# Token-by-token queries and keys in the last stage of a three-stage kernel, with longer loops on the matmul engine

## What is computed

```python
h = einsum('bhid,oi,od->bho', x, weighted_sum, weight)   # image tokens
h = concatenate([h, txt], axis=1)
h = h + attn(layernorm(h))     # 16 heads of 16; for each token position the 8 batch rows attend to each other
h = h + ffn(layernorm(h))

def ffn(x):                    # "last stage" below
    h = rmsnorm(x, gamma1)
    q = (h @ Wq + bq).reshape(b, t, H, HD)
    kv = ((h @ Wdown + bdown) @ Wup + bup).reshape(b, t, H, 2 * HD)
    k, v = split(kv, 2, axis=-1)
    att = softmax(einsum('bthd,btgd->bthg', q, k) / sqrt(HD))   # heads of one token attend to each other
    out = einsum('bthg,btgd->bthd', att, v).reshape(b, t, D)
    x = x + (out @ Wo + bo)
    h2 = rmsnorm(x, gamma2)
    gate = softmax(h2 @ Wg + bg)
    return x + einsum('btd,edf,bte->btf', h2, We, gate)         # 8 experts
```

## Time and profile before

| | us |
|---|---|
| median of 3 runs | 808.26 (807.35 to 809.14) |
| the profiled execution | 807.2 |
| its span (first to last instruction) | 805.3 |
| PE busy | 764.3 |
| DVE busy | 663.1 |
| POOL busy | 405.5 |
| ACT busy | 374.0 |

### The profile page before, as it was taken

How to read it: one execution, slowest core, us unless ns; L and a number is a source line. 1 busy time by engine, 2 the same in 40 slices (tenths; PEclk the granted TensorE clock), 3 DMA queues, 4 the chain that set the end, 5 groups by cost and what they waited for, 6 DMA issues and landing times.

```text
span 805.3 us, 48234 instructions
## 1 busy us (share of the span) xinstructions
PE 764.3 (95%) x20274; PEld 532.5 (66%) x20274; DVE 663.1 (82%) x1591; ACT 374.0 (46%) x985; POOL 405.5 (50%) x1094
## 2 busy tenths in 40 slices
PE   4999979999999998878999999999999999999998
PEld 3888845677677675566656666666666666666664
DVE  5798676899999997767778778778778877877877
ACT  4477444565666565534433434434333343443321
POOL 1231354566665667534545555555565565555311
PEclk9999998999999999978999999999999999999999
DMA  9987000000000000000001001001101100100100
GB/s 331 333 239 226 3 3 4 2 0 0 0 0 0 0 0 2 16 13 17 26 20 26 19 20 26 23 16 26 26 13 26 26 19 20 26 23 17 29 15 20
DMA packets 38377, 33.25 MB, mean 41 GB/s; under 512 B 24786, under 2 KB 33570, under 8 KB 38314
## 3 DMA queue, kind: packets, MB, share of 16 engines
q1 hardware_dynamic: 38314, 32.35, 13.4%
HBM read 22.64 MB, written 4.83 MB: 34 GB/s over the span
## 4 chain that ended last, share of the span: by engine, by line
PE 59%; DVE 16%; issue 8%; POOL 3%; DVEq 1%; ACT 0%; POOLq 0%; ACTq 0%
PE bank L192 13%; PE bank L194 11%; PE bank L193 11%; PE bank L957 9%; PE bank L968 6%; DVE smax L435 2%; DVE k_t L466 2%; DVE ss L469 2%; PE bank L976 1%; DVE qn L460 1%; DVE q_t L464 1%; PE bank L995 1%; DVE on_t_l L444 1%; PE bank L275 1%; DVE on L428 1%
## 5 line engine op out<-in xcount | busy, mean ns | idle before, releaser
L192 PE MATMUL bank<-we_h,h_t_h 128*128 128x512 f16 x296 | 112.9, 382 | 1.1 <-DVE res L1277 0.9
L193 PE MATMUL bank<-we_l,h_t_h 128*128 128x512 f16 x296 | 112.2, 379 | 0.0
L194 PE MATMUL bank<-we_h,h_t_l 128*128 128x512 f16 x296 | 112.2, 379 | 0.0
L1277 DVE SCALAR_TENSOR_TENSOR acc<-bank,gate,acc 128x256 f32<-128x256 f32 x222 | 101.9, 459 | 3.9 <-PE bank L194 3.4
L1286 DVE TENSOR_REDUCE smax<-bank 128x16 f32<-128x512 f32 x37 | 25.6, 692 | 70.7 <-PE bank L957 70.7
L192 PE MATMUL bank<-tokw_h,x_t_h 128*128 128x256 f16 x256 | 70.8, 277 | 11.3 <-DVE x_t_l L690 11.3
L957 PEld LDWEIGHTS bank<-kv_t,fq_t 32*32 32x32 f32 x4736 | 71.3, 145 | 10.7 <-issue 10.7
L957 PE MATMUL bank<-kv_t,fq_t 32*32 32x32 f32 x4736 | 76.0, 225 | 1.8 <-issue 1.7
L193 PE MATMUL bank<-tokw_l,x_t_h 128*128 128x256 f16 x256 | 70.8, 277 | 0.0
L194 PE MATMUL bank<-tokw_h,x_t_l 128*128 128x256 f16 x256 | 70.8, 276 | 0.0
L968 PEld LDWEIGHTS bank<-fpr_t,v 32*32 32x32 f32 x4736 | 48.2, 104 | 22.9 <-issue 22.1
(11 more groups left out here) (223 smaller groups left out, 2243.0 us busy)
## 6 DMA issues: line engine op xcount, KB each, us to landing
xbuf<-in_x SPq DMA_DIRECT2D x32, 512.0 KB, 5.2
out<-res SPq DMA_DIRECT2D x36, 128.0 KB
we_s<-in_we SPq DMA_DIRECT2D x4, 512.0 KB, 7.1
inw<-in_in_w SPq DMA_DIRECT2D x1, 768.0 KB, 11.8
hn_t_h<-hn_r_h SPq DMA_TRANSPOSE x37, 2.3
hn_t_l<-hn_r_l SPq DMA_TRANSPOSE x37, 2.4
wrep<-in_w_rep SPq DMA_DIRECT2D x1, 512.0 KB, 4.4
h_all<-in_txt SPq DMA_DIRECT2D x1, 512.0 KB
```

The source lines that it names most:

```text
L192: nc.tensor.matmul(dst, a_h(c), b_h(c), start=start and c == 0, stop=False)
L193: nc.tensor.matmul(dst, a_h(c), b_l(c), start=False, stop=False)
L194: last = nc.tensor.matmul(dst, a_l(c), b_h(c), start=False, stop=stop and c == chunks - 1)
L1277: nc.vector.scalar_tensor_tensor(out=(res if e == E - 1 else acc)[:, :], in0=b_we[s % 2][:, k * D:(k + 1) * D], scalar=gate[p][:, e:e + 1] ...
```

## The change

Three things are changed.

1. In the last stage `fq_t` and `kv_t` lie token by token. A pair is now tokens 2p and 2p + 1. `fq_t` holds 16 heads of a token in a run, so the stationary operand is one run of 32 words; the transpose that writes it steps by 16 words from element to element. `kv_t` keeps its content (the same flat order), but is read with both tokens of a pair next to each other: 16 runs of 2 words, 32 words apart. The transposes into `v48` and `of` and the mask follow suit.
2. PE's loops: attention covers turns 2 to 33, the last stage 4 to 35. Turn 39, which is empty, goes (`end=`). For that the wait for `bvec` moves to turn 1 and the wait for `a_h` is dropped; instead DVE does `added` ahead of on_l, so that `a_onl` covers both.
3. Normalised rows of tiles 0, 1 and 2: ACT writes them at the end of turns 32, 33, 34; POOL's low halves for them stand at the start of its turns 33, 34 and 35, ahead of Newton's steps; `first_coefficients` comes in turns 28 to 31.

```diff
--- before.py
+++ after.py
@@ -36,7 +36,6 @@
 XT = 3
 MIX = 4
 MIX0 = 3
-HEAD = range(TILES - 4, TILES + 2)
 JOIN = TILES - 1
 AHEAD = 4
 WS = 256.0
@@ -61,7 +60,7 @@
     eng.wait_ge(sem, 1)
 
 
-def tiles_in_order(eng, body, back, ahead, unroll=2, last_ahead=None, start=None, tail=None):
+def tiles_in_order(eng, body, back, ahead, unroll=2, last_ahead=None, start=None, tail=None, end=None):
 
 
     first = -(-(back + 1) // unroll) * unroll
@@ -71,7 +70,7 @@
     with eng.Fori(first // unroll, first // unroll + turns) as g:
         for p in range(unroll):
             body(g * unroll + p, p)
-    for i in range(first + unroll * turns, TILES + back):
+    for i in range(first + unroll * turns, end or TILES + back):
         if tail:
             tail(i)
         else:
@@ -317,6 +316,8 @@
                 sums(i, p, 1)
 
             def rows(i, p):
+                if isinstance(i, int) and i == 1:
+                    pe.wait_ge(bvec_ready, 1)
                 if real(i, 2):
                     pe.wait_ge(a_xtl, i + 3)
                     wait(pe, a_qk, i + 1)
@@ -335,9 +336,6 @@
                     last.then_inc(a_xnps, 1)
                 if real(i, -2):
                     pe.wait_ge(a_onl, i - 1)
-                    wait(pe, a_h, i - 2)
-                    if isinstance(i, int) and i == 2:
-                        pe.wait_ge(bvec_ready, 1)
                     rows_times(b_out, on_h, on_l, lambda c: outw_h[:, c, :], lambda c: outw_l[:, c, :]).then_inc(a_out, 1)
 
             def body(i, p):
@@ -440,12 +438,13 @@
                                             ALU.subtract).then_inc(a_sub, 1)
                 if real(i, -2):
                     dve.wait_ge(a_onh, i - 1)
+                if real(i, -3):
+                    added(i - 3)
+                if real(i, -2):
                     wait(dve, a_out, i - 2)
                     nc.vector.tensor_tensor(on_l[:, :, :], b_ot[:, 0:D], on_h[:, :, :], ALU.subtract).then_inc(a_onl, 1)
                 if early:
                     divisor(i)
-                if real(i, -3):
-                    added(i - 3)
                 if real(i, 0):
                     dve.wait_ge(a_exp, i + 1)
 
@@ -842,7 +841,7 @@
         hn_r = [halves(f"hn_r{p}", [P, D]) for p in range(2)]
         fpr_t = sb("fpr_t", [P, H, 32])
         fq_t = sb("fq_t", [P, 32, H])
-        kv_t = sb("kv_t", [P, 32, 16])
+        kv_t = sb("kv_t", [P, H, 32])
         of = sb("of", [P, H, 32])
         x2 = sb("x2", [P, D])
         hx2 = [sb(f"hx2_{p}", [P, D]) for p in range(2)]
@@ -955,8 +954,8 @@
                     for j in range(4):
                         q = slice(32 * j, 32 * j + 32)
                         last = nc.tensor.matmul(b_s3[q, pair * 32:pair * 32 + 32],
-                                                fq_t[q, :, pair],
-                                                kv_t[q, :, pair],
+                                                fq_t[q, 2 * pair:2 * pair + 2, :].rearrange("r t h -> r (t h)"),
+                                                kv_t[q, :, 2 * pair:2 * pair + 2],
                                                 start=False, stop=True, skip_group_check=True)
                 return last
 
@@ -1212,14 +1211,13 @@
             def join(i):
 
                 p, t = i % 2, i - JOIN
-                if t in (-3, -2):
+                if t in (-4, -3, -2):
                     a_body(i, p)
-                    rows(t, p)
+                    rows(t + 1, 1 - p)
                 elif t == -1:
                     asked(t)
                     down(t)
                     a_body(i, p)
-                    rows(t, 1)
                 elif t == 0:
                     asked(t)
                     down(t)
@@ -1319,7 +1317,7 @@
                 combine(i, p, 0)
                 if real(i, 1):
                     dve.wait_ge(f_qpad, i + 2)
-                    nc.vector.transpose(fq_t[:, :, :].rearrange("r (h t) p -> r h (t p)", t=2), qpad[:, :, :])
+                    nc.vector.transpose(fq_t[:, :, :].rearrange("r t h -> r h t"), qpad[:, :, :])
                 combine(i, p, 1)
                 if real(i, -1):
                     dve.wait_ge(f_wo, i)
@@ -1332,15 +1330,15 @@
                 combine(i, p, 2)
                 if real(i, 1):
                     dve.wait_ge(f_kv, i + 2)
-                    nc.vector.transpose(kv_t[:, :, :].rearrange("r n p -> r (n p)"), b_kv[:, :]).then_inc(f_kvt, 1)
+                    nc.vector.transpose(kv_t[:, :, :], b_kv[:, :]).then_inc(f_kvt, 1)
                 combine(i, p, 3)
                 if real(i, 1):
                     dve.wait_ge(f_kvt, i + 2)
                     nc.vector.transpose(v48[1 - p][:, :, 0:32],
-                                        kv_t[:, :, :].rearrange("r n p -> r p n")).then_inc(f_qt, 1)
+                                        kv_t[:, :, :].rearrange("r g (p t) -> r p g t", t=2)).then_inc(f_qt, 1)
                 if real(i, 0):
                     dve.wait_ge(f_av, i + 1)
-                    nc.vector.transpose(of[:, :, :], b_o3[:, :].rearrange("r (p h t) -> r h t p", h=H, t=2)).then_inc(f_of, 1)
+                    nc.vector.transpose(of[:, :, :], b_o3[:, :].rearrange("r (t h) -> r h t", h=H)).then_inc(f_of, 1)
                 combine(i, p, 4)
                 if real(i, 0):
                     dve.wait_ge(f_of, i + 1)
@@ -1379,7 +1377,13 @@
             return body, join
 
         def ffn_pool(pool):
-            def body(i, p):
+            def low(i, p):
+
+                if real(i, 3):
+                    pool.wait_ge(f_hn, i + 4)
+                    nc.gpsimd.tensor_tensor(hn_r[1 - p][1][:, :], hn[1 - p][:, :], hn_r[1 - p][0][:, :], ALU.subtract).then_inc(p_hnl, 1)
+
+            def body(i, p, early=None):
                 if real(i, 1):
                     pool.wait_ge(f_qraw, i + 2)
                     wait(pool, f_qt, i + 1)
@@ -1403,13 +1407,12 @@
                     pool.wait_ge(f_x1, i + 1)
                     wait(pool, f_x2, i)
                     nc.gpsimd.tensor_tensor(x1b[:, :], x1[:, :], bo_s[:, :], ALU.add).then_inc(p_x1, 1)
-                if real(i, 3):
-                    pool.wait_ge(f_hn, i + 4)
-                    nc.gpsimd.tensor_tensor(hn_r[1 - p][1][:, :], hn[1 - p][:, :], hn_r[1 - p][0][:, :], ALU.subtract).then_inc(p_hnl, 1)
+                if early is None:
+                    low(i, p)
                 if real(i, AHEAD) and real(i, 0):
                     ffn_coefficients(pool, i + AHEAD)
 
-            return body
+            return body, low
 
 
 
@@ -1418,8 +1421,8 @@
             @block.tensor
             def _(pe):
                 turn, (body, join) = attn_pe(pe)[0], ffn_pe(pe)
-                tiles_in_order(pe, turn, 3, 3, last_ahead=4, start=-1, tail=join)
-                tiles_in_order(pe, body, 2, 3, start=3)
+                tiles_in_order(pe, turn, 1, 3, start=-1, tail=join, end=TILES + 2)
+                tiles_in_order(pe, body, 2, 1, start=3)
 
             @block.scalar
             def _(act):
@@ -1437,16 +1440,20 @@
             def _(pool):
                 coefficients(pool, early, IMG_TILES)
 
-                body, head = attn_pool(pool), ffn_pool(pool)
+                body, (head, low) = attn_pool(pool), ffn_pool(pool)
 
                 def tail(i):
 
-                    body(i, i % 2)
-                    if HEAD[0] - 4 <= i < HEAD[0]:
-                        first_coefficients(pool, i - HEAD[0] + 4)
-                    if i in HEAD:
-                        turn = i - HEAD[0] - 3
-                        head(turn, turn % 2)
+                    p, t = i % 2, i - JOIN
+                    if t in (-3, -2, -1):
+                        low(t, p)
+                    body(i, p)
+                    if t < -4:
+                        first_coefficients(pool, t + 8)
+                    if t == -1:
+                        head(t, p, True)
+                    if t in (0, 1, 2):
+                        head(t, p)
 
                 tiles_in_order(pool, body, 3, 3, start=-1, last_ahead=8, tail=tail)
                 tiles_in_order(pool, head, 2, 3, last_ahead=AHEAD, start=3)
@@ -1505,7 +1512,7 @@
         "wo": a["L0_ffn_Wo"], "g2": columns(a["L0_ffn_gamma2"]),
         "wg": a["L0_ffn_Wg"], "we": a["L0_ffn_We"],
         "ident_c": np.eye(P, dtype=np.float32),
-        "amask_c": mask(4, lambda n: n % 32 // B, lambda n: n % 32 // B), "fmask_c": mask(2, lambda n: n % 2, lambda n: n % 2),
+        "amask_c": mask(4, lambda n: n % 32 // B, lambda n: n % 32 // B), "fmask_c": mask(2, lambda n: n % 32 // 16, lambda n: n % 2),
         "bv": columns(a["L0_attn_in_proj_bias"][2 * D:]), "bo": a["L0_ffn_bo"], "bq": a["L0_ffn_bq"], "bg": a["L0_ffn_bg"],
         "biases": np.concatenate([a["L0_attn_in_proj_bias"], a["L0_attn_out_b"], a["L0_ffn_bq"], a["L0_ffn_bo"], a["L0_ffn_bg"],
                                   np.zeros(P * BC - NBIAS, np.float32)]).reshape(P, BC),
```

## The result

The changed kernel takes 773.19 us (median of 4 runs, 771.31 to 774.41) where the kernel before takes 807.81 (4 runs): ratio 0.957, 95% interval 0.954 to 0.961. The forecast was 780 (780.2 by its sum) with a range from 774 to 797. The profiled execution took 773.28 us, its span is 771.3.

What follows compares the result with a forecast made beforehand. PE was taken to set steady last-stage turns, DVE steady attention turns. From 807.2 us, -21.8 (scores) - 4.0 - 1.8 - 0.7 (loops) + 0.2 (rows) = -28.1 gave 779.1, or 780.2 as median; range 774 to 797.

Steps and rivals of the forecast that it cites:

- I take 1.37, the nearest row in shape and count: 0.59 saved per turn: Last stage's score burst: falls from 1.96 to the sums' 1.37 us, 37 x 0.59 = 21.8 us saved.
- Bounds for one burst: Last stage's score burst: 1.96 us if nothing changes, 1.37 if it equals the sums' burst.
- more from the loops than I took (772 to 775): PE's loops: a larger saving than forecast, total 772 to 775 us, chance 0.04.
- The rival on the weight side: Score burst: only the weight side was the cost, half of 0.59 saved, 10.9 lost, 791 us; chance 0.17.
- DVE's price: DVE's last-stage transposes: fq_t rises from 0.70 to 1.03 us, v48 falls from 1.03 to 0.70, net zero.
- The slower rival: Last stage: fq_t's stepped write makes DVE the end; at 3.5 us the total is 820; chance 0.04.
- The loops: PE's loop bounds: 4.0 at attention's exit, 1.8 at its entry, 0.7 at the last loop's exit saved.
- Turns 4 and 5: Attention loop's entry: these turns, 6.41 and 7.58, come from the loop at 12.2 together, 1.8 us saved.
- The exit: Attention turns 32 to 35: 34.2 us falls to 30.2, 4.0 saved (0 to 6.6).
- Turn 34 becomes the first behind the loop and gets the stall: Attention turn 34: takes the stall and the low clock, 9.0 us; 6.6 saved at the exit if it stays clean.
- The last exit: Last stage's loop exit: the 1.18 us stall moves from turn 34 to 36, 0.7 us saved (0 to 1.4).
- worth nothing by itself: Attention turn 35: removing PE's 2.33 us wait for the halves saves nothing alone, as POOL's chain ends the turn.

Runs made afterwards that it cites:

- e1: The kernel before with only the token-by-token fq_t and kv_t layout and its transposes and mask; 781.30 us, ratio 0.964.
- e3: The changed kernel with kv_t read with a step of 16 words again, fq_t still in one run; 796.01 us, ratio 0.984.
- e4: The changed kernel with fq_t read with a step of 16 words again, kv_t still in pairs; 797.61 us, ratio 0.985.
- e2: The changed kernel with the fq_t and kv_t layout undone, loops and rows kept; 800.55 us, ratio 0.988.
- e6: The changed kernel with both PE loops at their old bounds (4 to 31, 4 to 33); 780.73 us, ratio 0.967.
- e7: The changed kernel with PE's attention loop over turns 4 to 33 and the last stage's loop as before; 782.19 us.
- e8: The changed kernel with PE's attention loop over turns 2 to 31 and the last stage's loop as before; 781.10 us.
- e10: The changed kernel with v48 widened to a pitch of 64 words, so the sums' weights start at multiples of 32 words; 771.10 us.
- e15: The changed kernel with transposed probabilities written so that the sums read them as 16 pairs, 32 words apart; 772.20 us.
- e14: The changed kernel with the scores' moving operand read in one run of 32 words instead of 16 pairs; 770.53 us.
- e5: The changed kernel with the rows of tiles 0 to 2, POOL's low halves and first coefficients put back; 774.12 us, ratio 0.960.
- e9: The changed kernel with the attention loop at its old bounds (4 to 31), last stage's loop at 4 to 35; 779.87 us, ratio 0.965.

## Why the prediction was right and wrong

**The range and the size: wrong, by one term.** The step that failed reads "I take 1.37, the nearest row in shape and count: 0.59 saved per turn", and with it "Bounds for one burst". The burst is 1.22: 0.74 saved, 0.75 a turn by the maxima; 37 turns make 27.8 instead of 21.8, and e1 alone gives 27.1. 1.37 was no lower end. The kernel before had shorter bursts of 128: the attention sums in its turn 34, and the very sums of line 968 in last-stage turns 35 and 36, where no transposing DMA lands in them. From the timeline of PE (start, us)

```profile
328.88 1.28 PE L275 MATMUL bank<-vaug,pr_t 32*32 32x17 f32 x128
330.10 0.39 PE L192 MATMUL bank<-inw_h,xt_h 128*128 128x512 f16 x1
...
773.65 1.29 PE L968 MATMUL bank<-fpr_t,v 32*32 32x32 f32 x128
774.87 0.39 PE L192 MATMUL bank<-we_h,h_t_h 128*128 128x512 f16 x1
```

with 1.22 us from each burst to what follows it, over 17 columns in the first and 32 in the second. As long with half the columns says that columns don't set the pace there, and the second row says that the sums at 1.37 carry something else, which goes with that DMA. With either row as the burst the forecast would have been 37 x 0.15 = 5.6 us lower, 774.6, and the range would have begun as much lower, at 768. The measured time lies where the prediction put "more from the loops than I took (772 to 775)" at 0.04; that the number fits is mostly not its doing, since the loops gave about 1 us more and the bursts 6.

**The rival on the weight side** had 0.17 and a false form: e3 and e4 show that the slower side alone sets the pace. The full gain needed both edits; the trace of before could not show it, since it has no burst with one side stepped.

**DVE's price: right.** 1.04 and 0.69 were the values taken, and the idle time of DVE hid them. The Trainium skill's rule on a stepped destination (Vector Engine (DVE) Microarchitecture Reference, section 5.2: 1.7 to 2.5 ns a column instead of 1.05, so 0.65 to 1.45 more) holds at its lower end: (1.04 - 0.70) / 512 is 0.66 ns a column more than in a run. The page has its upper figure for a small step (24 words); at the 16 words here the lower one was measured. The slower rival (fq_t at 3.2 us) is off by a factor of three.

**The loops: near in sum (forecast 6.5 without the rows, measured 7.9 in e2 and 7.5 in e6), not in their terms.** Turns 4 and 5 gave 1.8, to the digit. The exit gave 7.0 instead of 4.0, nearer to the 6.6 that the prediction had for a clean turn 34: the step "Turn 34 becomes the first behind the loop and gets the stall" failed, since whether the first turn stalls seems to hang on where the loop ends in the fetched blocks (e7, e8), which the earlier beginning had moved. The last exit went as forecast: turn 34 gave 1.4 (13.27 to 11.07, less 0.75 for the burst), a wait of 0.74 us now stands in turn 36, and all behind turn 35 takes 0.9 more, so 0.5 net for 0.7.

These terms make 9.3. The rest of the trace takes that down to 6.2, in the main by 1.2 us lost before the first maximum and by 2.3 between attention turn 36 and last-stage turn 5, where 2.2 us were gained and six shorter bursts alone should give 4.5. I had both at zero, and they are not shown to be the loops' doing. e1, with the old loops, has the same shortfall there (64.65 us for 67.31). And code that runs once varies: in thirteen kernels with the same PE code up to there, attention turn 6 begins at 147.3 (e10) to 151.6 us (e15), and from turn 36 to last-stage turn 5 the seven of them with short bursts, the sums at their place and the same PE loops take 62.7 (e14) to 67.4 us (e15). A difference of 2 us in these stretches, of one execution each, says nothing about an edit. So reading an edit by its own turns and expecting the total to follow was wrong as a method: e7 and e8 gained 4.5 and 4.1 us in turns 32 to 35 and nothing in the total, both ends together 7.3.

**The rows: right in total, not in reason.** I wrote that they are "worth nothing by itself" because POOL's chain ends turn 35 either way. With the old loops that holds: 9.26 (e6, rows early) against 9.54 before. With the new ones e5 shows the wait on the path and 2.5 us for it. In the total it is 0.9 us and can't be told from none.

**Packets.** Twelve fewer were forecast: 47 to 35.

**Open.** How the landing DMA holds up the sums' burst for 0.13 us. Why one end of the attention loop moved alone gains nothing in the total. That the stalls' lengths follow the blocks' places is borne out by two kernels only, and what decides them beyond the first turn is not settled.

## What to carry to other kernels

Where small f32 matmuls come in bursts, read both operands in runs, or the moving one in pairs of neighbouring words; mending one side alone brought 0.03 us of 0.74. Let the engine with idle time pay for the layout (here DVE, 0.34 us up and 0.34 down). When bounding a burst, take the fastest burst of the same count in the whole trace, whatever its width, and look whether a DMA lands in the slower ones. Count written-out PE instructions around loops as streamed code: test loop bounds together, since one end alone may bring nothing; compare stretches of such code over several kernels; and keep a loop's body within what stays on the engine.

## What the runs showed of the hardware

- A burst of 128 f32 matmuls of 32 x 32 took 1.96 us with both operands stepped by 16 words, 1.93 with only the moving one stepped, 1.96 with only the stationary one, 1.22 with neither; run and pairs on the moving side are alike (e14, e15).
- A DVE transpose of 128 x 512 f32 took 0.70 us with both sides in runs, 1.03 to 1.05 with either side stepped word by word, 0.69 with the input in pairs; PSUM read with a step of 16 or 32 words took 0.67.
- A burst of 128 f32 matmuls of 32 x 32 by 32 columns took 1.33 to 1.37 us while a transposing DMA landed in it, and 1.22 without (turns 34 and 35 of the last stage in the changed kernel, 1.36 and 1.22).
- PE's loop of 1262 instructions, as the profile counts them, needed next to no code from memory once it ran (1 packet of 16 KB in 335 us); one of 1776 needed 46 in 200 us and made PE wait in each turn. The Trainium skill (Advanced Engine Details and Errata, ISA Cache) gives TensorE 128 KB in blocks of 256 instructions; packets of 0.77 MB / 47 = 16.4 KB agree with the block. By that size 2048 instructions (an estimate) would stay, so the 1776 and their uncounted waits should have fitted nearly, and did not.
- Waits for code of 1.46 and 2.08 us inside a burst were followed by the lower clock (0.81 and 0.83 of full over turns 32 and 33 before, 1.00 in both after), which doubled their price; so was a wait of 2.70 us for a DMA (0.70 in e5's turn 35). Others were not: 1.88 us for code in e7's turn 34, 2.33 us for the DMA in turn 35 before, 1.18 us in last-stage turn 34 before, all with 1.00 over the turn. What decides is not shown.
- Turn 32 behind the same PE code took 8.08 us at a clock of 1.00 in e6, with a wait for code of 2.06 us, and 9.40 us at 0.82 in e9, with one of 1.79.
